# An attention kernel with relative positions: three PSUM banks used in turn by scores, relative scores and turned-back outputs

## What is computed

```python
r = jnp.arange(S)                                     # S = 2048
idx = jnp.clip(r[None, :] - r[:, None], -M, M) + M    # M = 128
rpk, rpv = rel_k[idx], rel_v[idx]
content = jnp.einsum('bhqd,bhkd->bhqk', q, k)
relative = jnp.einsum('bhqd,qkd->bhqk', q, rpk)
scores = (content + relative) / jnp.sqrt(jnp.float32(hd))
w = jax.nn.softmax(scores, axis=-1)
out = jnp.einsum('bhqk,bhkd->bhqd', w, v) + jnp.einsum('bhqk,qkd->bhqd', w, rpv)
...
x = x + s * g        # s: out @ Wo.T + bo, g: silu of the experts' output
```

## Time and profile before

| | |
|---|---|
| Time, median of 3 runs | 2553.29 us (2551.48 to 2554.37) |
| The profiled execution | 2557.0 us, span 2555.4 us |
| TensorE busy | 2399.6 us, 94% |
| VectorE busy | 1864.6 us, 73% |
| ScalarE busy | 1676.0 us, 66% |
| GpSimd busy | 1031.4 us, 40% |
| Granted TensorE clock, mean over the span | 0.973 |
| One head in the middle, 1171.00 to 1231.60: TensorE, VectorE, ScalarE, GpSimd busy | 59.67, 50.64, 47.70, 26.27 us of 60.60 |

### The profile page before, as it was taken

The page is one execution under the profiler, slowest core; times in us unless marked ns, Lnnn a source line. Parts: engine busy times, 40 slices in busy tenths (PEclk is TensorE's granted clock), DMA queues, the critical chain, the costliest instruction groups (busy, mean ns, idle before and its releaser), DMA issues. The chain is left out here.

```text
span 2555.4 us, 47614 instructions
## 1 busy us (share of the span) xinstructions
PE 2399.6 (94%) x14704; PEld 1167.3 (46%) x14704; DVE 1864.6 (73%) x5113; ACT 1676.0 (66%) x3898; POOL 1031.4 (40%) x2491
## 2 busy tenths in 40 slices
PE   6837999999999999999999999999999998699998
PEld 3411444444444444444444444444444443566666
DVE  6658888888888888888888888888888881333333
ACT  4523777777777777777777777777777777221111
POOL 1233444444444444444444444444444436133332
PEclk8965999999999999999999999999999999899999
DMA  5668788777787777777777777777777752822221
GB/s 164 170 154 266 252 276 266 242 229 242 244 248 231 241 243 247 241 241 245 243 249 240 233 245 242 249 229 239 243 247 237 235 187 51 318 93 67 67 67 50
DMA packets 351154, 540.98 MB, mean 212 GB/s; under 512 B 30608, under 2 KB 259392, under 8 KB 350912
## 3 DMA queue, kind: packets, MB, share of 16 engines
q1 hardware_dynamic: 336880, 502.76, 63.6%
q0 software_dynamic: 14032, 35.24, 4.6%
HBM read 272.60 MB, written 269.43 MB: 212 GB/s over the span
## 5 line engine op out<-in xcount | busy, mean ns | idle before, releaser
L1097 DVE TENSOR_REDUCE part<-ps 128x1 f32<-128x512 f32 (+3 forms) x2048 | 1197.4, 589 | 328.9 <-PE ps L984 313.3
L1153 ACT ACTIVATE probs_T<-pst 128x512 f32<-128x512 f32 (+3 forms) x2048 | 1016.2, 523 | 369.3 <-PE pst L993 367.4
L984 PE MATMUL ps<-k_front,q_front 96*128 96x512 bf16 x2048 | 805.5, 394 | 26.2 <-DVE part L1095 1.9
L933 PE MATMUL pout<-probs_T,v_far 128*32 128x512 f32 (+3 forms) x4864 | 546.1, 535 | 0.9 <-ACT probs_T L1136 0.7
L847 POOL TENSOR_TENSOR left_T<-probs_T,left_mask 128x128 f32<-128x128 f32 x512 | 217.4, 427 | 604.1 <-ACT probs_T L1136 448.8
L984 PEld LDWEIGHTS ps<-k_front,q_front 96*128 96x128 bf16 x2048 | 197.3, 96 | 563.0 <-DVE part L1097 330.8
L993 PE MATMUL pst<-q_back,k_right 102*128 102x512 bf16 (+3 forms) x1024 | 350.9, 343 | 5.0 <-ACT probs_T L1153 4.1
L993 PE MATMUL pst<-q_back,k_left 102*128 102x512 bf16 (+3 forms) x1024 | 352.4, 344 | 3.0 <-ACT probs_T L1153 1.8
L1166 ACT ACTIVATE band<-band,negm 128x384 f32<-128x384 f32 (+1 forms) x512 | 308.3, 602 | 0.1
L1095 DVE CUSTOM_DVE_ANT_0 band<-ps,band 128x256 f32<-128x256 f32 (+2 forms) x704 | 299.3, 425 | 0.0
L933 PEld LDWEIGHTS pout<-probs_T,v_far 128*32 128x32 f32 x4864 | 163.6, 108 | 225.4 <-issue 195.2
(11 more groups left out here) (160 smaller groups left out, 2256.2 us busy)
## 6 DMA issues: line engine op xcount, KB each, us to landing
rel_scores<-rel SPq DMA_DIRECT2D x128, 1024.0 KB, 8.3
band_probs<-band SPq DMA_DIRECT2D x128, 768.0 KB, 4.0
pwin<-band_probs SPq DMA_DIRECT2D x128, 512.0 KB
band<-rel_scores SPq DMA_DIRECT2D x64, 768.0 KB, 6.6
band<-rel_scores SPq DMA_DIRECT2D x64, 576.0 KB, 5.4
w<-in_w_dram SPq DMA_DIRECT2D x16, 1024.0 KB, 15.4
band<-rel_scores SPq DMA_DIRECT2D x64, 128.0 KB, 5.7
q_terms<-terms SPq DMA_DIRECT2D x48, 128.0 KB
```

The lines of the kernel that those rows point to most:

```text
L933: return nc.tensor.matmul(pout[32 * g:32 * g + 32, c0:c1], values, probs, start=first, stop=False, skip_group_check=True)
L984: nc.tensor.matmul(ps1[u % 2][:, :], q_front[a.par][:, a.s * P:(a.s + 1) * P], k_front[a.par][:, u * CW:(u + 1) * CW], start=True, stop=Tr ...
L1097: ins = nc.vector.tensor_reduce(peak, src, AX_X, ALU.max)
L1153: ins = nc.scalar.activation(probs_T[t.s % 2][:, u * CW + c0:u * CW + c1], pst[u % 2][:, c0:c1], ACT.Exp, scale=SCALE)
```

## The change

The two banks of the scores and the bank `prel` become a ring of three, `pring`. A list `turns` writes down who takes a bank, in order: in a step the four scores, then the relative score, then (in step 4) the turned-back outputs. Each takes the next bank, and TensorE waits before it until the third before it has been read out: a score by VectorE, a relative score by ScalarE, the outputs by VectorE's normalisation.

Three pieces of work move. The pass of values stands between the third score and the third transposed score in every step (before, behind the second transposed score, in step 1 behind the third). The relative score and the turning back stand behind the fourth transposed score, ahead of the window's transposes. ScalarE copies the relative score behind the fourth exponential instead of the second.

```diff
-        ps1 = [ctx.enter_context(nc.psum_tensor(f"ps1_{i}", [P, 512], F32)) for i in range(2)]
+        pring = [ctx.enter_context(nc.psum_tensor(f"pring{i}", [P, 512], F32)) for i in range(3)]
...
-        prel = ctx.enter_context(nc.psum_tensor("prel", [P, 512], F32))
...
+        turns = []
+        for hb in range(HEADS):
+            for off in range(-NB if at_start(hb) else 0, 2 * NB + (LAG_O if at_end(hb) else 0)):
+                a, x, o = Step(hb, off), Step(hb, off + LAG_R), Step(hb, off - LAG_O)
+                turns += [("scores", a.n, a.s, u) for u in range(CH) if a.valid]
+                turns += [("relative", x.n, x.s)] if x.valid else []
+                turns += [("outputs", o.n)] if o.valid and o.s == NB - 1 else []
+        place = {use: i for i, use in enumerate(turns)}
+
+        def ring_bank(use):
+            return pring[place[use] % 3]
+
+        def ring_free(use):
+
+            if place[use] < 3:
+                return None
+            kind, *at = turns[place[use] - 3]
+            if kind == "scores":
+                return s1_used, 64 * at[0] + 4 * at[1] + at[2] + 1
+            if kind == "relative":
+                return r_evac, 16 * at[0] + at[1] + 1
+            return norm_done, at[0] + 1
...
-                            wait(pe, s1_used, a.count(64, 4 * a.s + u - 1))
-                            nc.tensor.matmul(ps1[u % 2][:, :], q_front[a.par][:, a.s * P:(a.s + 1) * P], k_front[a.par][:, u * CW:(u + 1) * CW],
+                            use = ("scores", a.n, a.s, u)
+                            wait_bank(use)
+                            nc.tensor.matmul(ring_bank(use)[:, :], q_front[a.par][:, a.s * P:(a.s + 1) * P], k_front[a.par][:, u * CW:(u + 1) * CW],
                                              start=True, stop=True).then_inc(s1_mm, 1)
+                        if u == 2 and w.valid:
+                            key_values()
                         if t.valid:
...
-                        if u == 1 and x.valid:
-
-                            if x.s == 0:
-                                pe.wait_ge(qf_in[x.par], x.count2(48, 48))
-                            wait(pe, r_evac, x.count(16, x.s))
-                            if t.s == LAG_O - LAG_T:
-                                wait(pe, norm_done, t.count(1, 0))
-                            nc.tensor.matmul(prel[:, 0:RELS], q_front[x.par][:, x.s * P:(x.s + 1) * P], con["rel_k"][:, :], start=True, stop=True).then_inc(r_mm, 1)
-                        if u == (2 if w.s == 0 else 1) and w.valid:
-                            key_values()
...
-                        if u == 2 and o.s == NB - 1 and o.valid:
-                            turn_back()
+                    if x.valid:
+                        relative()
+                    if o.s == NB - 1 and o.valid:
+                        turn_back()
...
-                        if u == 1 and x.valid:
+                        if u == CH - 1 and x.valid:
                             relative()
```

## The result

| | before | after |
|---|---|---|
| Time, median (range) of 4 runs each | 2553.83 us (2551.48 to 2556.22) | 2566.68 us (2565.24 to 2571.90) |
| The profiled execution | 2557.0, span 2555.4 | 2567.0, span 2565.4 |
| Ratio, with its 95% interval | | 1.005 (1.0035 to 1.0066) |

The forecast was 2572 in a range of 2526 to 2592, slower.

A forecast was written before the change was run, and what follows sets the result against it. TensorE was taken as the bound, waiting 3.07 us a head. After the change 3.78 would remain: +0.71 a head, +21 us over 30 heads, -2 for the last, added to the 2553.3 median: 2572 us, range 2526 to 2592.

The forecast's parts named there:

- pass of step 1: In step 1 the pass of values waits for the copy of the finished outputs: 0.04 us a head.
- What bounds the kernel, and the sum of its waits: TensorE is busiest (94%); its waits for VectorE sum to 3.07 us a head, all the change can win.
- The third score ahead: Third score before the pass: VectorE works during the pass; waits left at second scores are 0.97 us a head.
- Relative score in the ring: Third scores wait for ScalarE's relative copy in steps 2, 3, 4, 6, 7, 8: 0.75 us a head.
- Turned-back outputs: In step 5 the third score waits for VectorE's normalisation: 0.15 us a head instead of 0.43.
- The chain: Later relative copy delays GpSimd's mask and shift rows: TensorE loses 1.44 us in step 9, 0.43 in step 0.
- The start-up: The prologue, which waits for SyncE's transfers of relative scores, was held to be free of the change.
- Rival 1: The mask chain does not reach TensorE: 2529 us, or 2516 without the 0.43 also; chance 0.27.
- Rival 2: The relative score's bank becomes the bound in every step: 2638 us; chance 0.10.
- Rival 3: Cancellation: the stall comes at 1.0 and the score waits 0.25 smaller: 2551 us; chance 0.10.
- Rival 4: All waits go, the repeated gap being a lack of banks: 92 us won, 2461 us; chance 0.03.

The follow-up runs named there:

- Experiment 6: Kernel before with the ring of three alone, plus the turning back moved behind step 4's fourth transposed score: 2475.17 us, 0.9687 of before.
- Experiment 4: Changed kernel with the pass of values back at its old place, so the third score goes behind the pass again: 2549.16 us, 0.9972 of before.
- experiment 5: Kernel before with only the banks shared in a ring of three, all work at its old places: 2497.52 us, 0.9772 of before.
- experiment 1: Changed kernel with GpSimd building v_far two steps later, behind that step's mask: 2524.70 us, 0.9884 of before.
- 2: Changed kernel with one of the two instructions that build v_far moved two steps later: 2546.78 us, 0.9963 of before.
- experiment 3: Changed kernel with GpSimd's ends and sides put behind the shift rows and the next step's mask: 2503.46 us, 0.9795 of before.
- 8: Kernel before, no ring, with ScalarE's relative copy behind the fourth exponential and the turning back ending the step: 2652.54 us, 1.0380 of before.

## Why the prediction was nearly right

| per head | predicted | measured in after |
|---|---|---|
| second scores wait for VectorE | 0.97 | 0.96 |
| third scores wait for the relative copy | 0.75 | 0.66 |
| second score of step 5 waits for the relative copy | 0 | 0.03 |
| normalised outputs, step 5 | 0.15 | 0 |
| pass of step 1 | 0.04 | 0.07 |
| chain to step 9's third transposed score | 1.44 | 1.44 |
| chain to step 0's fourth transposed score | 0.43 | 0.50 |
| sum | 3.78 | 3.66 |
| less the waits of before (3.07) | +0.71 | +0.59 by these rows, +0.53 by the period |

- **What bounds the kernel, and the sum of its waits.** Right. Experiment 6 wins 2.46 of the 3.07 us a head, so most of the waits read from distances of starts were there to be won.
- **The third score ahead.** The 0.97 came out, step by step within 0.03, but its reason was wrong. The text gave part of the relief to VectorE working during the pass. Experiment 4 takes that away, and nine of ten waits stay to 0.01. What relieved them is the relative score behind the fourth, 0.11 of work more: seven of the ten waits of after are 0.11 or 0.12 below those told of before (0.20 to 0.08, 0.25 to 0.14, 0.30 to 0.19, 0.23 to 0.12, 0.23 to 0.11, 0.18 to 0.07, 0.13 to 0.02). The third *bank* gave the scores nothing in this order. Between a step's fourth score and the next second one stand the relative score and the first score, so the second score wants the fourth's bank, as it did with two banks. In the old order the turn is first, second, relative, third, fourth, and the second score wants the bank of the *third*, which VectorE left long ago: experiment 5 has no such wait at all. The prediction counted the release and never asked whose bank the second score takes. That its 0.97 held is in part luck: the 0.11 stood in its sum whatever the reason given beside it.
- **Relative score in the ring.** 0.06, 0.11, 0.17, 0.19, 0.13 in steps 2, 3, 4, 6, 7 against 0.07, 0.13, 0.18, 0.19, 0.14; the 0.04 of step 8 did not come. No more than that is behind the 0.09 missing.
- **Turned-back outputs.** Mis-sized, 0.15 for nothing. VectorE's two instructions end 2.46 behind the third transposed score of step 4 (1232.60 to 1235.06), not 2.6; they were put 0.15 too late. The third score goes at 1235.12, with no wait of its own to see. The second score, at 1234.83, takes the bank of step 4's relative score in the ring and waits 0.03 for that copy.
- **The chain.** Right in every link. GpSimd starts on the ends at 1184.50, 0.81 behind step 8's start at 1183.69 (predicted 0.80 and a signal); ScalarE goes at 6.32 (6.35), TensorE at 6.97 (7.01). Experiments 1, 2 and 3 show it to be the cause, in dose and in whole; 8 shows it without the ring.
- **The difference of 0.18 a head** is 0.12 from these terms and 0.06 from distances that the table leaves out, each within 0.05 of its usual length (the first scores of steps 0 and 1, for one, start 0.27 behind the window's last pair in before and 0.22 in after).
- **The start-up.** The prediction held the prologue to be free of the change, and there it failed: 5.85 us were gained before the first turning back. Timeline of before and then of after, TensorE in the prologue, at the second head's first relative score:

```profile
199.27 0.40 PE L1006 MATMUL prel<-rel_k,q_front 96*128 96x257 bf16 x1 [13.18 <-DMA q_front<-q_terms]
```

```profile
193.56 0.40 PE L966 MATMUL pring<-rel_k,q_front 96*128 96x257 bf16 x1 [9.13 <-DMA q_front<-q_terms]
```

5.7 of the 5.85 us lie before this matmul, which waits for a load of queries. The load's three transfers were issued from 178.30 on in after and from 179.29 on in before, and took 13.6 to 13.9 us from issue to landing against 17.0 to 18.5, while the relative scores of the prologue are written and read in the same stretch. The length of the wait alone tells nothing: in experiment 1 it is 13.17, as long as in before, and the matmul starts at 194.48. In the nine kernels other than before it starts between 193.56 and 196.75, and the transfers take 13.6 to 17.4 us, with no order that the ring or the moves would give. There is one profile of each kernel, so why before is the latest, and how much this moves from one execution to the next, stays open; no run was made for it. Without these 5.85 us the change would stand at about 2572.5. The miss of 6.4 us (12.9 measured between the medians, 19.3 predicted) is thus: start-up -5.85, the period's 0.18 over 28 heads -5.0, the end +1.6, and +2.9 since the profile of before lay that much further over its median than the profile of after. These parts have both signs, so that 2572 came as near as it did is in part luck.

- **The rivals.** Rival 1 (the chain does not reach TensorE) did not happen; experiment 3 is what it would have been, and there it gives 2503, lower than the 2516 told, in part since its start-up is earlier too (first turning back at 315.9). Rival 2 did not happen: only five steps have a third score that waits for the relative copy. Rival 3 (a stall of 1.0, smaller waits) did not happen: the stall came whole. Rival 4, all waits go, was given 0.03 for this change, and for this change that holds. But its mechanism is sound. The second-score waits disappear with the third bank and nothing else (experiment 5), and with the turning back set right the kernel comes to 2475, 14 us from the 2461 of rival 4. So the gap repeated in step after step was a lack of banks, with 0.9772 for the ring alone and 0.9687 with one move. The Trainium skill (Perfetto Trace Analysis, Optimization Strategy) says that such a repeated gap can mean too little PSUM for the next tile; these two runs agree, and the 1.0050 of the change shows that the order in which the banks are taken decides whether they help. Where the prediction let only the ring's new waits speak against this rival, it took them for a property of the ring. They belong to the order that was chosen with it: in the old order no third score waits for a relative copy.

So the large gain was there and was given back. Against the ring alone (experiment 5) the change has, per head: the chain +1.94, third scores waiting for the relative copy +0.66, second scores waiting for the fourth's bank +0.96, the pass +0.07 and step 5's second score waiting for the relative copy +0.03; it saves the second transposed scores' 0.68 and the 0.69 at the normalised outputs. Sum +2.29, the periods differ by 2.34.

## What to carry to other kernels

Take apart a change that gives an engine another buffer and moves work at the same time: here the buffer alone was worth 2.3%, with one fitting move 3.1%, and with all moves it was a loss of 0.5%. When a copy is moved later in an engine's list, follow who waits for it through the in-order engines that seem idle (GpSimd was 40% busy, and yet before the change its mask ended only 0.14 us ahead of the exponential that waits for it, 1187.00 against 1187.14), and put what others wait for ahead of what has four steps of time. In a ring of buffers, write down for each user whose buffer it takes: a third bank helps the second score only in the order in which it takes the third score's bank, and not the fourth's.

## What the runs showed of the hardware that was not expected

Little. Distances between starts of matmuls add up so exactly in this kernel that a stall of 1.44 us worked out from engine to engine was measured as 1.44, and halving its cause took out 0.69. What was not expected is the spread of one load in the prologue: its transfers take 13.6 to 18.5 us from issue to landing over the ten kernels of this study, and the matmul behind it starts between 193.56 and 199.27, which is 0.2% of the time.
